# Layer 0 of a two-layer recurrent kernel: bank reads ordered by lags, four shared PSUM banks, stationary values in column tiles, the mixing beside the attention, and one expert tile less

## The reference, cut to what matters

```python
# layer 0, s: attention in windows of 64 tokens, 16 heads of 16
qkv = xw @ qkv_w + qkv_b
attn = einsum('bnqhd,bnkhd->bnhqk', q, k) * scale + rel_pos_bias
s = (softmax(attn) @ v) @ proj_w + proj_b
# layer 0, f: 32 experts (256 -> 256 -> 256), top 1, at most 160 tokens each
y = einsum('ecf,efh->ech', silu(buf @ w_gate) * (buf @ w_up), w_down)
f = xt + where(accepted, y[slot] * gate, 0)
x = x + s * silu(f)
# layer 1, s: unit projections in the Fourier domain, bind, cumulative sum, unbind
# layer 1, f: 8 experts (256 -> 1024 -> 256), top 2, no limit on tokens
x = x + s1 * silu(f1)
```

## Time and profile before

| | us |
|---|---|
| median of 3 runs | 1408.3 |
| lowest and highest | 1405.17, 1408.84 |
| the profiled execution, its own time | 1408.23 |
| its span, first to last instruction | 1406.2 |
| mean granted TensorE clock | 0.90 of full speed |
| TensorE busy | 1176.0 (84%) |
| VectorE busy | 688.3 (49%) |
| ScalarE busy | 536.4 (38%) |
| GpSimd busy | 317.5 (23%) |

### The profile page before, as it was taken

One profiled execution on the slowest core, in us unless ns is written; L12 is line 12 of the kernel. 1 busy time (PEld: TensorE's weight loads), 2 busy tenths in 40 slices (PEclk: granted clock), 3 DMA queues, 4 the chain that ended last, 5 costly groups with the idle time before them and its releaser, 6 DMA issues.

```text
span 1406.2 us, 16596 instructions
## 1 busy us (share of the span) xinstructions
PE 1176.0 (84%) x6124; PEld 1013.1 (72%) x6124; DVE 688.3 (49%) x1553; ACT 536.4 (38%) x1065; POOL 317.5 (23%) x320
## 2 busy tenths in 40 slices
PE   4943789999999898665498999999999999999940
PEld 4822678777777686554387888888888888888930
DVE  7283457666666564876747565565460000000027
ACT  1311334333334332533305555565542332323444
POOL 1027000101000123540143223223232222322200
PEclk8776799999999999865659999999999999999975
DMA  9102222323333224344041343344255496645956
GB/s 326 58 23 99 69 88 93 105 90 101 102 96 92 82 84 140 111 138 139 1 191 52 143 173 134 125 173 151 106 206 215 173 374 242 225 169 211 337 171 209
DMA packets 97488, 204.40 MB, mean 145 GB/s; under 512 B 9982, under 2 KB 82176, under 8 KB 92288
## 3 DMA queue, kind: packets, MB, share of 16 engines
q1 hardware_dynamic: 83568, 166.66, 34.2%
q0 software_dynamic: 13840, 36.68, 7.4%
HBM read 162.71 MB, written 41.68 MB: 145 GB/s over the span
## 4 chain that ended last, share of the span: by engine, by line
PE 64%; DVE 11%; ACT 6%; issue 6%; DMA 3%; SPq 2%; POOL 2%; another core or an unknown queue 0%; POOLq 0%; ACTq 0%; DVEq 0%
PE PS L926 16%; PE PS L916 15%; PE PS L855 6%; PE PS L814 4%; PE PS L774 4%; PE PS L752 3%; PE PS L827 2%; PE PS L824 2%; PE PS L762 2%; PE PS L878 2%; PE PS L795 2%; PE PS L730 2%; PE PS L739 1%; ACT L1664 1%; DVE sc L1116 1%
## 5 line engine op out<-in xcount | busy, mean ns | idle before, releaser
L916 PE MATMUL PS<-xgT,WE 128*128 128x256 f32 (+1 forms) x1280 | 262.0, 361 | 7.3 <-ACT hT L1664 4.6
L926 PE MATMUL PS<-WE,hT 128*128 128x256 f32 x1152 | 255.2, 379 | 0.0
L916 PEld LDWEIGHTS PS<-xgT,WE 128*128 128x128 f32 x1280 | 222.9, 191 | 39.6 <-ACT hT L1664 10.6
L926 PEld LDWEIGHTS PS<-WE,hT 128*128 128x128 f32 x1152 | 216.8, 190 | 28.4
L1664 ACT ACTIVATE hT<-PS,WE 128x256 f32<-128x256 f32 (+1 forms) x320 | 141.4, 452 | 238.0 <-PE PS L916 223.7
L1460 DVE TENSOR_TENSOR y<-PS,WE 128x512 f32<-128x512 f32 (+1 forms) x40 | 25.5, 638 | 399.7 <-PE PS L926 399.7
L1769 POOL DMA_INDIRECT result<-y,result_of x72 | 71.9, 999 | 300.3 <-DVE y L1460 290.6
L1557 ACT ACTIVATE prob<-sc 128x512 f32<-128x512 f32 x64 | 40.3, 630 | 187.4 <-DVE sc L1123 141.8
L1712 POOL DMA_DIRECT2D result<-y x32 | 18.1, 564 | 335.3 <-DVE y L1172 335.3
L855 PE MATMUL PS<-XT,Wf 128*128 128x256 f32 x384 | 90.4, 394 | 0.6 <-ACT Z L1628 0.6
L855 PEld LDWEIGHTS PS<-XT,Wf 128*128 128x128 f32 x384 | 75.1, 199 | 11.4 <-ACT Z L1628 1.0
(11 more groups left out here) (221 smaller groups left out, 1799.6 us busy)
## 6 DMA issues: line engine op xcount, KB each, us to landing
WE<-in_experts SPq DMA_DIRECT2D x40, 2180.0 KB
X<-in_x SPq DMA_DIRECT2D x16, 512.0 KB, 6.3
wgt<-in_w_gate SPq DMA_DIRECT2D x32, 256.0 KB, 2.9
wgt<-in_w_up SPq DMA_DIRECT2D x32, 256.0 KB, 3.5
wgt<-in_w_down SPq DMA_DIRECT2D x32, 256.0 KB, 2.7
both<-result SPq DMA_DIRECT2D x16, 512.0 KB, 8.8
table<-zeros POOLq DMA_DIRECT2D x1, 5120.0 KB, 22.1
rows<-table SPq DMA_DIRECT2D x40, 128.0 KB, 2.3
```

The source lines that it names most:

```text
L916: m = e.matmul(PS[:, FIRST_H_BANK + nth % HR, 0:rows], W1[n % WR][:, k, c * P:(c + 1) * P], xgT[:, n % 2, k, 0:rows], start=k == 0, stop=k ...
L926: m = e.matmul(PS[:, u.bank, j * D:(j + 1) * D], hT[:, n % 2, c, j * P:(j + 1) * P], W2[n % WR][:, c, :], start=c == 0, stop=c == KF - 1)
```

## The change

It rewrites the order and the operations of layer 0, and takes one tile from layer 1.

- **Order.** What reads a bank is now an item of its own (`q_out`, `k_out`, `v_out`, `score_out`, `exp`, `share`, `pt_out`, `even`, `odd`, `s_out`, `rows_out`, `tanh`, `gate`, `y_out`), put into the list when a clock of TensorE columns has passed the product by a lag. The products other than score and gu go round four banks.
- **Softmax.** GpSimd does every subtraction. VectorE sums the rows of the probabilities and takes the reciprocal (`share`), GpSimd multiplies the probabilities by it, before the transposes.
- **Values.** v is stationary (64 columns) in column tiles 0 and 64, the transposed probabilities move (128 columns). The result comes out transposed: the second transpose (785), its copy and the scaling (1132, 1141) go. ScalarE copies the even heads, VectorE adds the odd ones. The bias of v goes through `proj_w` into `proj_b`, once, in `fold`. ScalarE copies half of v.
- **Experts.** One expert per step; gate and up of an expert are one item over banks 4 and 5, with one tanh and two VectorE products of 320 columns.
- **Mixing.** silu is x/2 (1 + tanh(x/2)), with one half in s already. The combination starts behind the last expert and goes on beside the attention, one piece in each half step. Its product with s moves to GpSimd.
- **Layer 1.** 39 slots, 71 tiles. An eighth single tile would go to the last pair slot.

```diff
-PAIR_SLOTS, SINGLE_SLOTS = T * TOPK // (2 * P), E1
+PAIR_SLOTS, SINGLE_SLOTS = T * TOPK // (2 * P), E1 - 1
...
+    def product(self, what, *at, bank=None, columns, frees=1, then):
+        bank = self.spare() if bank is None else bank
+        for item in self.last.get(bank, ()):
+            self.need(item)
+        self.add(what, *at)
+        self.banks.take((what, *at), bank, frees)
+        self.clock += columns
+        self.last[bank] = [(name, *at) for name, _ in then]
+        for name, lag in then:
+            self.later(lag, (name, *at))
+SPARE = (2, 3, 6, 7)
...
+    def score(s):
+        need(("q_out", s // UW))
+        need(("k_out", s // UW))
+        order.product("score", s, bank=s % 2, columns=4 * UT, then=[("score_out", 100), ("exp", 3700), ("share", 4600)])
+    def pturn(s):
+        need(("share", s))
+        order.product("pturn", s, columns=4 * P, then=[("pt_out", 100)])
...
+        for q in range(QUARTERS):
+            add("mix_gate", q)
+            yield
+            add("mix_silu", q)
+            yield
+            while 4 * q + 3 not in projected:
                 yield
+            need(("s_out", 4 * q + 3))
+            add("mix_add", q)
+            if q + 2 < QUARTERS:
+                add("mix_gather", q + 2)
+            yield
+            if q % 2:
+                g = 4 * (q - 1)
                 add("stats", 1, g)
                 yield
                 add("norm", 1, g)
                 yield
+                turn(1, g)
+                yield
+                route1(g)
+                yield
...
+    def side(s):
+        if not advance(first):
+            return
+        if s >= FIRST_EXPERT_STEP and advance(ffn):
+            advance(combine)
...
+    for s in range(STEPS + 4):
+        if s + 2 < STEPS:
+            score(s + 2)
+        if u + 1 < UNITS and g < 3:
+            (q, k, v)[g](u + 1)
+        side(s)
+        if s % 2 == 0 and 0 <= s - 2 < STEPS:
+            pv((s - 2) // 2)
+        if s % 2 and 0 <= s - 3 < STEPS:
+            proj((s - 3) // 2)
+            projected.add((s - 3) // 2)
+        side(s)
+        if s < STEPS:
+            pturn(s)
...
+            u = use["vp",]
+            for c in range(KD):
+                m = e.matmul(PS[:, u.bank, 0:D], v_rep[:, c, :], proj_w[:, c, :], start=c == 0, stop=c == KD - 1)
...
+                        cols = slice(64 * (i % 2), 64 * (i % 2) + 64)
+                        m = e.matmul(out_v[cols, i // 2, :, win, :],
+                                     VB[:, unit % 2, 2 * j + win, i, :, :].rearrange("p g n -> p (g n)"),
+                                     PT[:, t % 2, win, i, :].rearrange("p (e q) -> p e q", e=2), start=True, stop=True)
...
+            elif what == "share":
+                s, = at
+                w.wait_ge(exp_done, s + 1)
+                w.wait_ge(prob_ready, s - RR + 1)
+                e.tensor_reduce(row_sum[:, s % RR, :], prob[:, s % PR0, :, :], AX.X, ALU.add).then_inc(row_sum_done, 1)
+                w.wait_ge(row_sum_done, s + 1)
+                e.reciprocal(row_sum[:, s % RR, :], row_sum[:, s % RR, :]).then_inc(inv_sum_done, 1)
...
+            elif what == "fold":
+                u = use["vp",]
+                filled_by(u)
+                e.tensor_tensor(proj_b[:, :], PS[:, u.bank, 0:D], proj_b[:, :], ALU.add).then_inc(free[u.bank], 1)
+                w.wait_ge(free[u.bank], u.emptied)
+                e.tensor_scalar(proj_b[:, :], proj_b[:, :], 0.5, None, ALU.mult).then_inc(proj_b_ready, 1)
...
+            elif what == "mix_silu":
+                q, = at
+                w.wait_ge(gated0, q + 1)
+                e.scalar_tensor_tensor(out=got0[:, q % 2, :, :], in0=mix_tanh[:, :, :], scalar=1.0, in1=got0[:, q % 2, :, :],
+                                       op0=ALU.add, op1=ALU.mult).then_inc(silu_ready, 1)
...
-            elif what == "score":
+            elif what == "score_out":
                 s, = at
-                if s >= DVE_BUSY_STEP:
+                w.wait_ge(sc_max_done, s + 1)
+                e.tensor_tensor(by_head, by_head, sc_max[:, s % SR, :].unsqueeze(2).to_broadcast([P, PAIRS, WIN]),
+                                ALU.subtract).then_inc(sc_sub_done, 1)
+            elif what == "share":
+                s, = at
+                w.wait_ge(inv_sum_done, s + 1)
+                e.tensor_tensor(prob[:, s % PR0, :, :], prob[:, s % PR0, :, :],
+                                row_sum[:, s % RR, :].unsqueeze(2).to_broadcast([P, PAIRS, WIN]),
+                                ALU.mult).then_inc(prob_ready, 1)
...
+            elif what == "mix_add":
+                q, = at
+                w.wait_ge(silu_ready, q + 1)
+                e.tensor_tensor(got0[:, q % 2, :, :], got0[:, q % 2, :, :], S[:, 4 * q:4 * q + 4, :], ALU.mult).then_inc(
+                    scaled0, 1)
```

More of the change, by code:

```diff
@@ new lines, with __init__, settle, need @@
+class Order:
+    def __init__(self, banks):
+        self.banks, self.plan, self.clock, self.late = banks, [], 0, []
+        self.last, self.turn = {}, 0
+    def settle(self, until):
+        while self.late and self.late[0][0] <= until:
+            self.plan.append(self.late.pop(0)[2])
+    def need(self, item):
+        for due, _, pending in list(self.late):
+            if pending == item:
+                self.settle(due)
+    def add(self, what, *at):
+        self.settle(self.clock)
+        self.plan.append((what, *at))
+    def later(self, columns, item):
+        self.late.append((self.clock + columns, len(self.plan) + len(self.late), item))
+        self.late.sort()
+    def spare(self):
+        self.turn += 1
+        return SPARE[self.turn % len(SPARE)]
+    def take(self, item, bank):
+        for read in self.last.pop(bank, ()):
+            self.need(read)
+        self.banks.take(item, bank)
+    def product(self, what, *at, bank=None, columns, frees=1, then):
[8 more added lines that the diff above has]
+            self.later(lag, (name, *at))
@@ L169, in normalized, with fold, route0_count @@
     def normalized(layer, g):
         add("norm", layer, g)
-        add("turn", layer, g)
+        turn(layer, g)
+    def fold():
+        for n in range(3):
+            for c in range(KD):
+                order.take(("wf", n, c), c)
+        order.take(("bf",), 2)
+        order.take(("vp",), 3)
+        add("fold")
+    def route0_count():
+        for i in range(2):
+            order.take(("before0", i), 4 + i)
+            order.take(("total0", i), 6 + i)
+        add("route0_count")
@@ L173, in start, with route1 @@
+    def route1(g):
+        order.take(("route1", g), 4)
+        add("route1", g)
     def start():
@@ L195, in experts @@
         for n in range(GT):
-            add("rows", n)
+            rows(n)
             if n % 2:
```

464 lines of the change are left out of this document (205 added, 259 removed).

## The result

The changed kernel takes 1420.41 us (median of five runs, 1417.54 to 1423.85), the kernel before 1405.17 beside it: ratio 1.0084, 95% interval 1.0065 to 1.0102. Forecast were 1385.0 and faster; it is slower. (The ratios are those on record; they are not the quotients of two medians, which here would be 1.0108.) Two later groups of runs, each with the kernel before beside it, gave 1.0174 (1.0144 to 1.0205) and 1.0038 (1.0017 to 1.0060). So the sign holds, and the size differs from group to group by more than one interval says.

A forecast was written before the change was run, and what follows sets the result against it. Layer 0 was held bound by TensorE beside the experts, then by VectorE's mixing and hand-overs. Layer 1 starting 16 us earlier, -7.5 for a slot and +0.4 gave -23 from 1408.2: 1385 us, range 1356 to 1420.

The forecast's parts named there:

- To the release of GpSimd: Beginning of layer 0: the last scatter is issued, freeing GpSimd for the softmax, at 142 us; it was 137.8.
- together 4.2 (bounds 1 and 6): Beginning: delay from transposes waiting for `fold` (about 2.7) plus exposed copies of v and a fill (some 1.5).
- Steps 0 to 6: Attention steps before the experts: 5 us filling and 5.0 per step, so step 7 starts at 182; 25 lost.
- Steps 7 to 39: Attention with one expert per step: 273 us including 5 for step 7, plus 3 of waits, ending at 458.
- (c): Rival in the value products: two column tiles run side by side, values at half price, -15, 1370 us; chance 0.08.
- Steps 40 to 58.5 and the end: Mixing beside attention, 148 us to 606, then remaining steps, 28; from last down product to last proj 176.
- To 118 I add three waits: Mixing: VectorE's 118 us plus add behind GpSimd's product 17, collisions 5, first gate's gathers about 8: 148.
- (a): Rival in the mixing: VectorE and GpSimd serialize, +39 there, early steps +7, 1431 us; decides from 9.2 per step; chance 0.18.
- The end: After the last proj, up to layer 1's first product at 651: product, add, statistics, normalizations, transposes, router, 17 us.
- Layer 1: One single slot less gives -7.5 us, two small VectorE instructions in the slot computation +0.4.
- (b): Rival in the mixing: it runs without added waits, 118 us for 148, total 1355; chance 0.14.
- (d): Rival in the expert steps: banks and lags change little, 0.77 us per step stays lost, +21, 1406; chance 0.10.

The follow-up runs named there:

- the controls: The changed kernel itself, unedited, run again in two later groups: 1417.76 us (ratio 1.0174 to the kernel before) and 1416.73 us (1.0038).
- moving eight steps: Changed kernel with the softmax subtraction and multiplication of steps 0 to 7 on VectorE instead of GpSimd: 1399.11 us, ratio 0.9917 to the kernel before.
- tiles apart: Changed kernel with a tile's eight value products ordered four on column tile 0, then four on column tile 64: 1427.22 us, ratio 1.0228.
- all the edits: Changed kernel with beginning's VectorE order restored, early softmax on VectorE, ScalarE's tanh and root later, gathers apart, product with s on VectorE: 1362.16 us, ratio 0.9673.

## Why the prediction was wrong

*To the release of GpSimd* (forecast 142, measured 148.1; 144.2 and 144.5 in the controls). The term that was mis-sized is "together 4.2 (bounds 1 and 6)": it was 10.3, and 6.4 and 6.7 in the controls. The wait for `fold` and the exposed copies and fill are there as described (0.84 and 0.91 us). Missing were the logits' copies, which wait in VectorE's queue ahead of statistics (L1115, 8.38; 5.62 and 5.53 in the controls) and make `fold` begin 2.4 and 2.7 later than before in the controls. The other 3.7 us in this execution go with TensorE's lower clock ahead of `fold`. The diff shows the copy with lag 0 behind its product, and the text costed only what stood behind `fold`.

*Steps 0 to 6*: 42.3 us for a forecast 40. Right, and undone by moving eight steps (23.5 us in this stage). The forecast of a loss here was its best new term.

*Steps 7 to 39*: 263 for 276. Waits were as small as said. The term that was mis-sized is values at 1.83 "I keep", which is 1.02; (c), given 0.08, was true. The Trainium skill's statement in TensorEngine Tiling (Array Packing), Key Properties, that different tiles can execute in parallel, was named and given little weight because no row showed it; with tiles apart at 1.51 and alternating at 1.02 the runs agree with it. The forecast's own sum of it, -15, was measured as -13.

*Steps 40 to 58.5 and the end* (forecast 176, measured 208). This step made the sign wrong. The step that failed is "To 118 I add three waits": it took VectorE's work as a floor with a few waits on top. VectorE's volume was nearly right: 118 and 6.5 steps of 3.5 make 141 of work, and 133 was measured. Its idle time was 75 and not 35. The three waits came out somewhat larger: the add behind GpSimd 20.0 for 17, the first gate 11.3 for 8, and the collisions some 10 for 5. Half of these are eight times 1.86 less 1.23 of the row below (1225 ns in the run with the mixing behind the attention). The rest is in the gates (528 ns for 478), the normalizations (494 for 416) and three small instructions (527 for 171); GpSimd's products of the softmax add 4 us on their side (1118 and 1141 for 1042).

```profile
L1269 DVE SCALAR_TENSOR_TENSOR got<-mix_tanh,got 128x1024 f32<-128x1024 f32 x8 | 14.9, 1857 | 1.8 <-ACT mix_tanh L1708 1.8
```

What no term held is ScalarE, and with it 32.4 us in which VectorE waits for its copies and exponentials. The text counted ScalarE's work nowhere in this stage, and its queue carries tanh and root, which wait for VectorE, ahead of exponentials that VectorE's sums and GpSimd's products wait for. So a wait on one queue delays a round through three of them. That this loop is what makes the waits grow is argued from the traces; what the edits show is its size in parts. Moving ScalarE's items alone gave back 6.8 us of the 32, and all the edits (four of order, and the product with s on VectorE) took the stage with its end from the control's 229.2 us to 202.7 without removing an instruction from it.

The forecast's 176 + 17 is 193. With the product on VectorE its own terms would give 186 (17 us of waits less, 9.8 of work more), so 17 us stay open. In that run VectorE still waits 25.1 us for ScalarE (15.0 and 10.1), for which the sum had no term. A rival that no run tests is TensorE's clock: side by side TensorE is busy 140.3 us in 454 to 682 where the two parts have 89.0 + 31.9, and each of its products that VectorE or ScalarE waits for is so much longer.

*The end*: 20.4 for 17, of it 2.82 a wait for the weights of layer 1. *Layer 1*: 736 for 732. The single slot is as forecast. The other 4 us are in part the first products of the experts, which run at a granted clock of 0.74 (755 to 775 us) where the kernel before had 0.91 at the same distance from layer 1's first product. Why is open: TensorE had been busy for two thirds of the 73 us before that in both kernels. The controls have 735.0 and 733.2.

*The rivals.* (a), serialization of VectorE and GpSimd, came closest in time (1431) and is not the cause. GpSimd's 64 products with the reciprocal have a mean of 1074 ns and a median of 1043, so they don't collide throughout, and moving one product off GpSimd shortened the stage although the collisions grew. The Trainium skill's lock (SBUF — State Buffer, Who interferes with whom) is seen in single rows: silu at 1.86 in the mean, once 3.82. All collisions together lengthen VectorE's instructions by some 10 us and GpSimd's by 4. The 9.2 us per step from which (a) was to decide do not follow from its own sum: 18.5 steps and 8 us on top reach 148 + 23 at 8.8. (b) has no support. (d) is refuted by the first window above.

The chance of slower was 0.19, and its only named mechanism was (a). A second way to be slower, the mixing and the softmax waiting for each other by order through ScalarE's queue, was not among the rivals.

## What to carry to other kernels

When work is moved beside other work on in-order queues, list for each engine, ScalarE too, the items that wait for another engine and what stands behind them; busy shares say only what the sum could be. Test an overlap by laying the two parts end to end: here 107 + 124 against 228.5 showed at once that it hid nothing. A copy out of a bank that is listed right behind its product makes its in-order engine wait for the product, and what that engine owes to others waits with it. Take a second profile of the same kernel before a difference of a few us is put down to the order: here the last scatter ended at 144.2, 144.5 and 148.1.

## What the runs showed of the hardware

- Two 128 x 64 column tiles in fp32 with alternating products: sixteen instructions of 128 columns in 1.02 us; the same sixteen, eight on one tile and then eight on the other, in 1.51.
- Three comparisons of the same two kernels gave 1.0084, 1.0174 and 1.0038, each with an interval of about 0.002 to 0.003 to either side. Two groups of runs on one chip (number 9) had the kernel before at 1396.2 and 1409.7 in the median. So the interval speaks for its group of runs alone.
- GpSimd's product of 128 x 1024 elements took 2.34 us, over twice its 128 x 512 (1.04 undisturbed), and the same on VectorE 1.21.
- Beside the mixing, VectorE's product of two 128 x 1024 inputs with silu had a mean of 1.86 us for 1.23, and GpSimd's 128 x 512 products 1.12 to 1.14 for 1.04; with one more such product on VectorE 1.20 to 1.23.
- With the mixing alone TensorE's granted clock was 0.56 in 559 to 683 us, with the attention alone 0.96 just before it, and 0.75 in 454 to 682 us with both side by side: the overlapped stage pays TensorE's work at the lower level in part, too (140.3 us busy against 89.0 + 31.9).
